# GpSimd issues its 32 row gathers in groups of four, and waits for the fourth's landing before it begins the next group

## The chip, the core and the metric

The kernel runs on one core of a Trainium2 chip. A core has a matrix engine (TensorE, PE in the profile), a vector engine (VectorE, DVE), a scalar engine (ScalarE, ACT), GpSimd (POOL) and SyncE (SP); each has its own instruction stream, and they wait for one another by semaphores. Sixteen DMA engines move data between the core's memory and the chip's main memory. The metric is the device time of one execution in microseconds (us); less is better.

## The reference

The function is one decoder layer on x of 4 x 256 tokens, 256 wide, in float32:

```
x = x + attention(layernorm(x))          # 16 heads of 128, weights = codes * scales
x = x + routed_mlp(layernorm(x), token)  # one of 4 experts, chosen by the token's id
x = x + moe(layernorm(x))                # below

scores  = sigmoid(xs @ router_w.T)
_, idx  = top_k(scores + bias, 4)                 # 4 of 32 experts for each of 1024 tokens
w       = scores[idx] / sum(scores[idx])
out     = sum over experts e of  mlp_e(xs) * w_e  # silu(x@wg) * (x@wu) @ wd, 256 -> 128 -> 256
out     = out + shared_mlp(xs)
```

The change lies in the last part, the mixture of 32 experts. It computes the experts only on the rows that chose them: 1024 tokens x 4 choices = 4096 rows.

## The kernel before, in words

The expert part is sorted by expert. The normalised tokens are stored in main memory as `h_dram`. The table `source` says for each of the 4096 places, in the order of the experts, which token stands there. GpSimd fetches the rows with 32 indirect DMAs (`ROWS = 32`), 128 rows of 256 floats (128 KB) each; I call them row gathers, numbered 0 to 31. Each goes to one of eight slots (`STEPS = 8`) of the tile `xg`, which shares its memory with `x_in`, so the profile calls it `x_in`. Each slot has a semaphore `d_g[n % 8]`, and a landed gather adds 16 to it.

TensorE takes the rows two gathers at a time: `turn_rows(p)` waits until gathers 2p and 2p + 1 have landed, turns them with four transposes (line 1386), and adds 1 to `t_x` after each gather. I call p a pair, 0 to 15. ScalarE copies the turned pair to `xT_all` (`row_copy`, line 1708). Gather n writes over the slot of gather n - 8, so GpSimd waits ahead of gather n for `t_x >= n - 7`.

The experts run as 24 steps b (`NB = 24`), each of 4 x 64 rows. For a step, VectorE copies the rows it needs (`unit_copies`, line 2113) and the weights of the odd experts (`gate_weights`, line 2121). TensorE does the gate and up products (`gate_up_unit`, lines 1399 and 1401, which count up `t_gu`); ScalarE does the silu (line 1652); VectorE multiplies (line 1982); TensorE turns the result (line 1411) and does the down product (lines 1422 and 1425); ScalarE copies it out (line 1662), and SyncE stores it to `y_dram`. Pairs 0 and 1 are turned ahead of the steps, and the table

```
TURN_PAIRS = {0: (2,), 1: (3,), 2: (4,), 3: (5,), 4: (6,), 5: (7, 8), 6: (9,), 7: (10, 11), 8: (12,), 9: (13, 14), 10: (15,)}
```

says behind which step TensorE turns which pairs. TensorE goes through its list in order, so a pair that isn't there holds up the steps behind it.

GpSimd's own list behind the row gathers: eight gathers of `x_all` from `x2_dram` (line 877; the profile calls the source `x_dram`). The first waits for the store that SyncE issues at its step 6, and each for a count of `t_gu`. Then 32 result gathers of `yg` from `y_dram` (line 898), each of which waits for steps to have finished. At the end VectorE and TensorE sum four results per token.

Of the kernel before, what the change touches and what calls it, by code (L numbers as in the profile page):

```python
# [45 lines left out]
HALVES = (T * TOPK + NE * (HS - 1)) // HS + 1  # L46
UNITS, NB = HALVES // 2, HALVES // 4
STEPS = 8
PACK = 4
ROWS = T * TOPK // SLOTS  # L50
PAIRS_OF_ROWS = ROWS // 2
# [2 lines left out]
HOT = NT // 2  # L54
assert NB * PACK == HALVES == 96 and STEPS == 2 * PACK and (2 * NB - 3) % 3 == 0
CH = TOPK * NT
# [6 lines left out]
def wait(eng, sem, value):  # L63

    if isinstance(value, int) and value <= 0:
        return
    eng.wait_ge(sem, value)


def apart(eng):  # L70


    eng.nop(nofuse=True)
# [132 lines left out]
def decoder_layer(nc, a, out):  # L206
    ctx = ExitStack()
    with ctx:
# [3 lines left out]
        def sem(name):  # L212
            return ctx.enter_context(nc.semaphore(name))
# [236 lines left out]
        t_x, v_x = sem("t_x"), sem("v_x")  # L450
        d_g = [sem(f"d_g{u}") for u in range(STEPS)]
        d_y = [sem(f"d_y{u}") for u in range(3)]
# [230 lines left out]
        def _(pool):  # L683
# [183 lines left out]

            for n in range(ROWS):
                wait(pool, t_x, n - STEPS + 1)
                pool.indirect_dma_start(out=xg[:, n % STEPS, :], out_offset=None, in_=h_dram,  # L870
                                        in_offset=bass.IndirectOffsetOnAxis(ap=source[:, n:n + 1], axis=0),
                                        bounds_check=T - 1, oob_is_err=False).then_inc(d_g[n % STEPS], 16)

# [120 lines left out]
        def _(pe):  # L994
# [163 lines left out]

            at = [pe.alloc_register(f"at{i}") for i in range(STEPS)]

            def load_kinds(w):

                apart(pe)
                pe.reg_load(at[w % 2 * PACK:w % 2 * PACK + PACK],
                            seg_expert[0:1, :, :].rearrange("p h i -> p (h i)")[:, w * PACK:(w + 1) * PACK])

# [195 lines left out]
            def load_experts(word):  # L1362

                for i in range(2):
                    into = at[i * PACK:(i + 1) * PACK] if word == 0 else ahead[(2 * word - 2 + i) * PACK:(2 * word - 1 + i) * PACK]
                    apart(pe)
                    start = 2 * i * NB + word * PACK
                    pe.reg_load(into, column_of[0:1, start:start + PACK])

# [922 lines left out]
```

## Time and profile before

| | |
|---|---|
| median of 3 runs | 535.88 us (534.71 to 536.13) |
| the profiled execution, its own time | 529.36 us |
| its span, from first to last instruction | 527.6 us |
| around the span | 1.76 us |
| granted TensorE clock, mean | 0.968 of full speed |
| TensorE busy | 476.5 us, 90% |
| VectorE busy | 386.4 us, 73% |
| ScalarE busy | 290.9 us, 55% |
| GpSimd busy | 203.0 us, 38% |
| the DMA queue of GpSimd's gathers and scatters | 3936 packets, 10.55 MB, 6.8% of 16 engines |

The profiled execution is 6.5 us shorter than the median of the timed runs, so a difference that is worked out from the trace is added to the median, and the trace's own total isn't compared with it. Busy time is not the same as need: each engine works through its list, and what matters is which wait ends last at each place. A time in square brackets in a row is idle time ahead of an instruction, with what ended it; "remote" and "another core or an unknown queue" mean that the profile knows no instruction of this kernel that ended it. The row gathers lie between 380 and 435 us of the span, the `x_all` gathers between 438 and 449, the result gathers between 457 and 512.

### The profile page before, as it was taken

The page shows a single profiled execution, that of the slowest core. Times are in us where ns is not written, and L with a number is a line of the kernel's source. Part 1 is how long each engine was busy: PE and PEld are TensorE (multiplying, and loading weights), DVE is VectorE, ACT ScalarE, POOL GpSimd, SP SyncE. Part 2 cuts the span into 40 slices and gives each one's busy share as a digit, 9 for nine tenths or more (in the row PEclk, how much of TensorE's full clock was granted, in tenths as well). Part 3 has the DMA queues.
Part 4 walks back from the last instruction along what each step waited for, and adds up shares of the span by engine and source line. Part 5 has one row for each costly group of instructions (what it writes and reads, how often), then busy time and mean ns, then how long its engine had stood idle before and what let it go on. Part 6 is the DMA issues. An engine that isn't in the chain of part 4 may idle for free.

```text
span 527.6 us, 11508 instructions
## 1 busy us (share of the span) xinstructions
PE 476.5 (90%) x3407; PEld 403.4 (76%) x3407; DVE 386.4 (73%) x997; ACT 290.9 (55%) x750; POOL 203.0 (38%) x248
## 2 busy tenths in 40 slices
PE   6899999999999999999999999899867988848848
PEld 6688999998998999999999998798734554424425
DVE  5689979879889879789888886887936863525415
ACT  2677667656667656667566655564323544423332
POOL 4418604404305215124122245253174655265250
PEclk9999999999999999999999999999996999987888
DMA  7342211201202203102005912999732455243334
GB/s 195 117 115 60 71 31 33 79 19 53 74 2 61 69 0 84 45 26 74 0 0 180 329 47 85 253 311 295 222 101 70 141 163 179 94 140 111 110 119 141
DMA packets 60662, 56.72 MB, mean 107 GB/s; under 512 B 4896, under 2 KB 57968, under 8 KB 60528
## 3 DMA queue, kind: packets, MB, share of 16 engines
q1 hardware_dynamic: 55984, 45.18, 28.8%
q0 software_dynamic: 3936, 10.55, 6.8%
q10 hardware_dynamic: 704, 0.52, 0.3%
q8 instruction: 18, 0.29, 0.2%
q14 instruction: 20, 0.16, 0.1%
HBM read 45.72 MB, written 16.81 MB: 119 GB/s over the span
## 4 chain that ended last, share of the span: by engine, by line
PE 72%; DVE 8%; another core or an unknown queue 6%; issue 5%; ACT 3%; POOL 3%; DVEq 1%; DMA 1%; ACTq 1%; SPq 0%; POOLq 0%
PE bank L997 18%; PE bank L998 17%; PE bank L999 17%; PE bank L1078 5%; PE bank L1399 4%; PE bank L1422 3%; PE bank L1003 1%; PE bank L1475 1%; POOL h_row L748 1%; DVE gate_of_odd L2121 1%; PE bank L1411 1%; PE bank L1425 1%; PE bank L1386 1%; POOL xs_dram L817 1%
## 5 line engine op out<-in xcount | busy, mean ns | idle before, releaser
L708 POOL TENSOR_TENSOR w_lo<-st_c,w_hi 128x512 fp32r<-128x512 f32 x32 | 41.4, 1293 | 175.1 <-ACT w_hi L1488 175.1
L1525 ACT ACTIVATE prob<-bank,nmax 128x256 f32<-128x256 f32 x128 | 59.6, 471 | 74.2 <-DVE nmax L1810 73.7
L1399 PE MATMUL bank<-moe_w,xT 128*64 x192 | 51.9, 411 | 16.2 <-DVE gate_of_odd L2121 15.1
L1810 DVE TENSOR_REDUCE nmax<-bank 128x2 f32<-128x512 f32 x64 | 44.1, 689 | 23.8 <-PE bank L999 23.8
L1825 DVE TENSOR_SCALAR prob<-prob,rinv 128x256 f32<-128x256 f32 x128 | 57.6, 491 | 2.3
L1802 DVE SCALAR_TENSOR_TENSOR qk_lo<-bank,b_col,qk_hi 128x512 fp32r<-128x512 f32 x64 | 47.7, 745 | 14.5 <-ACT qk_hi L1517 14.5
L1517 ACT ACTIVATE qk_hi<-bank,b_col 128x512 fp32r<-128x512 f32 x64 | 44.0, 688 | 22.1 <-PE bank L999 20.9
L997 PE MATMUL bank<-hT_hi,w_lo 128*128 128x512 f32 x128 | 51.3, 401 | 1.4 <-DVE qk_lo L1802 1.2
L1399 PEld LDWEIGHTS bank<-moe_w,xT 128*64 128x64 f32 x192 | 25.4, 145 | 35.3 <-issue 26.6
L1401 PE MATMUL bank<-gate_of_odd,xT 128*64 128x256 f32 x192 | 51.9, 411 | 0.2 <-issue 0.2
L998 PE MATMUL bank<-hT_lo,w_hi 128*128 128x512 f32 x128 | 50.7, 396 | 0.0
L999 PE MATMUL bank<-hT_hi,w_hi 128*128 128x512 f32 x128 | 50.4, 394 | 0.0
L870 POOL DMA_INDIRECT x_in<-h_dram,source x32 | 33.1, 1034 | 39.1 <-DVE source L2065 18.1
L1982 DVE TENSOR_TENSOR hid<-bank,sg 128x256 f32<-128x256 f32 x24 | 10.1, 421 | 50.2 <-ACT sg L1652 43.1
L1832 DVE TENSOR_TENSOR pT_lo<-bank,pT_hi 128x512 fp32r<-128x512 f32 x64 | 43.5, 680 | 0.6 <-ACT pT_hi L1542 0.6
L898 POOL DMA_INDIRECT yg<-y_dram,y_slot x32 | 30.7, 959 | 31.7 <-issue 20.6
L705 POOL TENSOR_TENSOR st_c<-st_c,st_s 128x512 f32<-128x512 f32 x32 | 41.8, 1305 | 1.3
L997 PE MATMUL bank<-pT_hi,v_lo 128*128 128x256 f32 x128 | 41.1, 321 | 0.5 <-DVE oT_lo L1840 0.5
L1422 PE MATMUL bank<-moe_w,hidT 128*64 x96 | 29.5, 439 | 10.5 <-issue 7.7
L1542 ACT CAST pT_hi<-bank 128x512 fp32r<-128x512 f32 x64 | 38.1, 595 | 0.7 <-PE bank L1078 0.7
L1078 PE MATMUL bank<-ident,prob 128*128 128x128 f32 x256 | 38.4, 272 | 0.0
L997 PE MATMUL bank<-qk_hi,qk_lo 128*128 128x256 f32 x128 | 36.6, 286 | 0.8 <-DVE qk_lo L1802 0.8
(288 smaller groups left out, 1546.1 us busy)
## 6 DMA issues: line engine op xcount, KB each, us to landing
y_dram<-ysb SPq DMA_DIRECT2D x24, 256.0 KB
moe_w<-in_w_gate SPq DMA_DIRECT2D x8, 512.0 KB, 8.3
moe_w<-in_w_up SPq DMA_DIRECT2D x8, 512.0 KB, 7.8
moe_w<-in_w_down SPq DMA_DIRECT2D x4, 1024.0 KB, 8.7
st_c<-in_wq_codes SPq DMA_DIRECT2D x16, 128.0 KB
st_c<-in_wk_codes SPq DMA_DIRECT2D x16, 128.0 KB
st_c<-in_wv_codes SPq DMA_DIRECT2D x8, 256.0 KB
st_c<-in_wo_codes SPq DMA_DIRECT2D x8, 256.0 KB
```

The lines of the kernel that those rows point to most:

```text
L997: pe.matmul(o, l_lo, r_hi, start=start, stop=False, skip_group_check=share)
L998: pe.matmul(o, l_hi, r_lo, start=False, stop=False, skip_group_check=share)
L999: return pe.matmul(o, l_hi, r_hi, start=False, stop=stop, skip_group_check=share)
L1078: mm = pe.transpose(bP[i % 2][:, kt * S + qt * P:kt * S + qt * P + P], prob[:, i % 4, qt, kt * P:kt * P + P], ident[:, :])
L1399: pe.matmul(o[0:HS, :], rows[:, 0:HS], weights_of(even_expert(b, i), kt * 2 * FI, 2 * FI), start=kt == 0, stop=kt == KT - 1, skip_group_ch ...
L1401: mm = pe.matmul(o[HS:SLOTS, :], rows[:, HS:SLOTS], gate_of_odd[:, (2 * b + i) % 3, kt * 2 * FI:(kt + 1) * 2 * FI], start=kt == 0, stop=kt ...
L1422: pe.matmul(o[0:HS, :], columns[:, 0:HS], weights_of(even_expert(b, i), 2 * D, D), start=True, stop=True, skip_group_check=True)
L1517: act.activation(qk_hi[:, hp, m, n * HALF:(n + 1) * HALF], src[:, :], ACT.Identity, bias=b_col[:, bass.ds(g_h + m * H, 1)]).then_inc(a_qk, 1)
L1525: ex = act.activation(prob[:, i % 4, qt, :], bS[i % 2][:, qt * S:(qt + 1) * S], ACT.Exp, bias=nmax[:, i % 2, qt:qt + 1], scale=-1.0, accum ...
L1802: dve.scalar_tensor_tensor(out=qk_lo[:, hp, m, n * HALF:(n + 1) * HALF], in0=src[:, :], scalar=b_col[:, bass.ds(g_h + m * H, 1)], in1=qk_h ...
L1810: dve.tensor_reduce(nmax[:, i % 2, :], bS[i % 2][:, :].rearrange("p (q k) -> p q k", q=2), AX.X, ALU.min).then_inc(v_max, 1)
L1825: sc = dve.tensor_scalar(prob[:, j % 4, qt, :], prob[:, j % 4, qt, :], rinv[:, j % 2, qt:qt + 1], None, ALU.mult)
```

## The change

The gathers are issued in the same order, from the same engine, to the same slots. Before gathers 4, 8, 12, 16, 20, 24 and 28, GpSimd now also waits until the gather right ahead (3, 7, 11, ...) has landed. That makes seven new waits. The `x_all` gathers and the result gathers have no new wait.

```
@@
 STEPS = 8
+BURST = 4
 PACK = 4
@@
             for n in range(ROWS):
                 wait(pool, t_x, n - STEPS + 1)
+                if n and n % BURST == 0:
+                    pool.wait_ge(d_g[(n - 1) % STEPS], 16 * ((n - 1) // STEPS + 1))
                 pool.indirect_dma_start(out=xg[:, n % STEPS, :], out_offset=None, in_=h_dram,
                                         in_offset=bass.IndirectOffsetOnAxis(ap=source[:, n:n + 1], axis=0),
                                         bounds_check=T - 1, oob_is_err=False).then_inc(d_g[n % STEPS], 16)
```

## Rows read from the trace of the kernel before

**Rows 1.** Page, part 4: the chain that ended last, shares of the span.
```profile
PE 72%; DVE 8%; another core or an unknown queue 6%; issue 5%; ACT 3%; POOL 3%; DVEq 1%; DMA 1%; ACTq 1%; SPq 0%; POOLq 0%
```
**Rows 2.** Chain, 388 to 400 us and 425 to 427: start, length, what.
```profile
388.97 9.18 another core or an unknown queue
...
399.54 0.68 PE bank L1399
400.24 0.41 PE bank L1399
...
425.94 0.20 PE bank L1399
```
**Rows 3.** Timeline of GpSimd: start, length, line, operation [idle before].
```profile
380.78 1.20 POOL L870 DMA_INDIRECT x_in<-h_dram,source  x1 [18.09 <-DVE source L2065]
...
384.89 1.00 POOL L870 DMA_INDIRECT x_in<-h_dram,source  x1 [0.30 <-issue]
386.20 1.00 POOL L870 DMA_INDIRECT x_in<-h_dram,source  x1 [0.30 <-issue]
...
395.34 1.00 POOL L870 DMA_INDIRECT x_in<-h_dram,source  x1 [0.30 <-issue]
398.94 1.00 POOL L870 DMA_INDIRECT x_in<-h_dram,source  x1 [2.60 <-remote]
...
429.96 1.00 POOL L870 DMA_INDIRECT x_in<-h_dram,source  x1 [1.51 <-PE bank L1386]
...
433.87 1.00 POOL L870 DMA_INDIRECT x_in<-h_dram,source  x1 [0.30 <-issue]
438.80 0.97 POOL L877 DMA_INDIRECT x_all<-x_dram,dest  x1 [3.93 <-DMA x_dram<-x_all]
...
447.60 0.95 POOL L877 DMA_INDIRECT x_all<-x_dram,dest  x1 [0.30 <-issue]
...
479.58 0.95 POOL L898 DMA_INDIRECT yg<-y_dram,y_slot  x1 [0.30 <-issue]
...
510.71 0.95 POOL L898 DMA_INDIRECT yg<-y_dram,y_slot  x1 [0.30 <-issue]
```
**Rows 4.** Timeline of ScalarE.
```profile
449.56 0.59 ACT L1708 COPY xT_all<-bank 128x512 f32<-128x512 f32 x1 [3.91 <-remote]
...
481.58 0.38 ACT L1652 ACTIVATE sg<-bank 128x256 f32<-128x256 f32 x1 [4.38 <-remote]
...
513.44 0.38 ACT L1652 ACTIVATE sg<-bank 128x256 f32<-128x256 f32 x1 [7.36 <-remote]
```
**Rows 5.** Timeline of TensorE's weight loads (the second half of pair 1).
```profile
387.80 0.20 PEld L1386 LDWEIGHTS bank<-ident,x_in 128*128 128x128 f32 x2 [0.44 <-DMA x_in<-h_dram,source]
```
**Rows 6.** Timeline of TensorE's matmuls: pair 2, pairs 7 and 8, pairs 13 and 14.
```profile
390.81 0.66 PE L1386 MATMUL bank<-ident,x_in 128*128 128x128 f32 x4
...
418.06 1.04 PE L1386 MATMUL bank<-ident,x_in 128*128 128x128 f32 x8
...
437.19 1.04 PE L1386 MATMUL bank<-ident,x_in 128*128 128x128 f32 x8
```
**Rows 7.** Windows: us, PE, PEld, DVE, ACT, POOL busy (x), PEclk, DMA share, GB/s.
```profile
386.00:391.00 5.00, 4.01 (x30) 2.43 (x29) 3.52 (x13) 2.08 (x5) 3.89 (x4) 1.00 0.36 104
...
394.00:395.00 1.00, 0.00 (x0) 0.00 (x0) 0.00 (x0) 0.00 (x0) 0.96 (x1) 1.00 0.41 119
...
404.00:405.00 1.00, 1.00 (x8) 0.62 (x6) 0.96 (x3) 0.00 (x0) 0.69 (x2) 0.50 0.00 0
...
431.00:436.00 5.00, 4.64 (x41) 2.56 (x39) 1.42 (x7) 2.48 (x7) 3.00 (x3) 1.00 0.81 263
```
**Rows 8.** Timeline of SyncE: the store that the `x_all` gathers wait for.
```profile
431.85 0.36 SPq L669 DMA_DIRECT2D x_dram<-x_all  x1
```
**Rows 9.** DMA issues of the page: operation, count, KB each, us to landing.
```profile
x_dram<-x_all SPq DMA_DIRECT2D x1, 1056.0 KB, 6.7
```
**Rows 10.** Timeline of VectorE: the table of the gathers.
```profile
379.67 0.19 DVE L2065 TENSOR_SCALAR source<-bank 128x32 int32<-128x32 f32 x1 [0.19 <-PE bank L1346]
```

More of the change, by code:

```diff
@@ L48 @@
 STEPS = 8
+BURST = 4
 PACK = 4
@@ L869, in _ @@
                 wait(pool, t_x, n - STEPS + 1)
+                if n and n % BURST == 0:
+                    pool.wait_ge(d_g[(n - 1) % STEPS], 16 * ((n - 1) // STEPS + 1))
                 pool.indirect_dma_start(out=xg[:, n % STEPS, :], out_offset=None, in_=h_dram,
```

## The prediction, as put on record before the changed kernel ran

> **What bounds the kernel now.** I read the chain of waits first. TensorE has 72% of it, and 6% is "another core or an unknown queue" [rows 1]. A piece of that kind lies right where the row gathers run: ScalarE does nothing for 9.18 us from 388.97, then does its first silu, VectorE multiplies, and TensorE can go on at 399.54 [rows 2]. No instruction of the kernel ends this stall. So I looked at what ends beside it.
>
> GpSimd's timeline shows twelve row gathers in an unbroken row, from 380.78 until the twelfth, which begins at 395.34 and takes 1.00 us; then it too is idle for 2.60 us until a "remote" event [rows 3]. ScalarE wakes at 388.97 + 9.18 = 398.15, that is 1.8 us after GpSimd stopped. The same shape returns three times. ScalarE begins at 449.56 after 3.91 us of "remote" idleness, and the last `x_all` gather ended at 447.60 + 0.95 = 448.55; it begins at 481.58, a group of result gathers ended at 480.53; it begins at 513.44, the last result gather ended at 511.66 [rows 3, 4]. So ScalarE wakes 1.0, 1.05 and 1.8 us after a run of gathers stops. My reading is that something that ScalarE needs from memory, most likely its next block of instructions, doesn't come while GpSimd issues gathers back to back, and comes in a pause. The rows show the coincidence, not the cause.
>
> **The price of one new wait.** Back to back, gathers begin 1.31 us apart (384.89 to 386.20) [rows 3]. Gather 3 begins at 384.89, and TensorE, which waited for it, begins at 387.80 [rows 3, 5]. So a row gather lands 2.9 us after its start. This was beside 104 GB/s of traffic; later the gathers share the engines with stores, up to 263 GB/s and a DMA share of 0.81 [rows 7], and I take 3.0 on the mean. For the upper end, nothing shows a gather's landing there; I take one us more, 3.9.
>
> From the landing to the next gather's start, two rows bound the price. The store of 1056 KB was issued at 431.85 and took 6.7 us to land, so at 438.55, and GpSimd began at 438.80: 0.25 us [rows 3, 8, 9]. The table `source` was ready at 379.67 + 0.19 = 379.86, and GpSimd began at 380.78: 0.9 us [rows 3, 10]. I take 0.5, since the first of the two is itself a wait on a landing. A group of four then takes 3 x 1.31 + 3.0 + 0.5 = 7.4 us. With both low ends it is 3.9 + 2.9 + 0.25 = 7.1, with both high ends 3.9 + 3.9 + 0.9 = 8.7.
>
> The Trainium skill ("DMA: Bandwidth & Descriptors", Anatomy of one DMA) puts a DMA from GpSimd at about 2.0 us plus bytes over 436 GB/s, which for 128 KB is an estimate of 2.3 us. The row has 2.9 from the start of the issue, and the sum goes by the row. By the page, a group would take 6.7 us and the whole would end near 530.
>
> **The new timetable of the gathers.** Gather 4 begins at 384.89 + 2.9 + 0.5 = 388.3 instead of 386.20 [rows 3]. The further groups begin 7.4 us apart: 395.7 (gather 8), 403.1, 410.5, 417.9, 425.3 and 432.7 (gather 28). Before, gather 28 began at 429.96 and gather 31 at 433.87 [rows 3]; now gather 31 begins at 432.7 + 3.9 = 436.6, which is 2.7 later. The old waits on `t_x` ask for pairs that TensorE turned long ago by then and add nothing.
>
> **What the early part gains.** The pause after gather 7 lasts from 388.3 + 3.9 + 1.0 = 393.2 to 395.7. If ScalarE wakes 1.8 us into a pause, it wakes at 395.0 instead of 398.15: 3.2 us earlier. Pair 2 (gathers 4 and 5) now lands at 388.3 + 1.3 + 2.9 = 392.5 instead of being turned at 390.81 [rows 6], but TensorE then waits for ScalarE in any case, so this is hidden; without that cover it would cost 1.7 us.
>
> The clock adds to it. It was full at 394 to 395 and half (0.50, so 1.2 GHz) at 404 to 405, after TensorE had been idle [rows 7]; the pieces of line 1399 took 0.41 us there and 0.20 at full clock [rows 2]. TensorE does about nine such steps and six transposes between 399.54 and 405. A shorter idle time may spare the fall: 9 x 0.21 + 6 x 0.1 = 2.5 us. So TensorE could be 3.2 to 5.7 us early when it comes to the later pairs.
>
> **Where that gain ends.** Two places hold it back, both by the timetable.
>
> First, TensorE's turns. Pair 8 needs gather 17, which lands at 410.5 + 1.3 + 3.0 = 414.8, and was turned in the second half of the row at 418.06: 3.8 us of slack. Pair 14 needs gather 29, which lands at 432.7 + 1.3 + 3.0 = 437.0. It was turned in the second half of the row at 437.19, so from 437.7 [rows 6]. The slack is 0.7 us. However early TensorE is, it gets past pair 14 only 0.7 us earlier than before.
>
> Second, the `x_all` gathers, which stand behind gather 31 in GpSimd's list. The store that they wait for would come early too, but GpSimd is free at 436.6 + 1.0 + 0.3 = 437.9. They begin 0.9 us earlier than at 438.80 [rows 3] and take as long as before. ScalarE's stall that ended at 449.56 ended 1.0 us behind them [rows 4], so it ends 0.9 earlier. Behind it, each step and the result gathers move as one.
>
> The sum: up to 5.7 us gained at 400, of which 5 are given back by 438, and 0.8 us remain. On the profiled execution's own time that is 529.36 - 0.8 = 528.6 us; the median lies 6.5 us above that execution, and I put the difference on it: 535.88 - 0.8 = 535.1 us. A difference within 0.3% (1.6 us) is no change that a measurement of this kernel can tell, so this forecast is "no change".
>
> **Rival 1, faster: the groups follow one another quickly.** With 7.1 us per group, gather 28 begins at 388.0 + 6 x 7.1 = 430.6. Gather 29 lands at 434.8, so pair 14 comes 2.9 us earlier, and the `x_all` gathers begin at 435.8, 3.0 earlier. Time: 532.9 us. For it: the low ends are both from waits on landings. Against it: the stores. A stronger form is that one of ScalarE's later stalls, such as the 3.91 us [rows 4], also gets shorter because its fetch falls in another pause: up to 530 us.
>
> **Rival 2, slower: the chain of landings gets longer than TensorE's need.** The place is pair 14 and the first `x_all` gather; it decides once a group takes more than about 7.55 us, since then 388.3 + 6 x 7.55 + 5.2 passes 438.8. With a landing of 3.4 and a wake of 0.7 a group takes 8.0 us. Gather 28 begins at 388.5 + 48 = 436.5, gather 29 lands at 441.2 (3.5 us late), and the `x_all` gathers begin at 441.7 (2.9 late). Time: 535.9 + 3.1 = 539.0 us; at 8.7 us per group it would be 543. For it: the DMA share of 0.81 around 433 [rows 7], and nothing else that limits the last groups.
>
> **Rival 3: a pause doesn't end ScalarE's stall.** Then it lasts to 398.15 as before, the groups' waits are covered by the slack of 0.7 us and more, and the time stays at 535.9 us, or some tenths above. For it: GpSimd's own 2.60 us of "remote" idleness [rows 3] could have the same foreign cause as ScalarE's stall, instead of being its end. The Trainium skill ("DMA: Bandwidth & Descriptors", Queues, rings and completion order) speaks for this rival: each DMA engine takes turns between its queues packet by packet, so that a fetch wouldn't have to wait for the gathers to pause. By that page nothing is gained at 389. The four coincidences above speak against it.
>
> **Chances.** The forecast, a gain that the timetable takes back: 0.35, no change. Rival 1: 0.33, faster. Rival 2: 0.22, slower. Rival 3: 0.10, of which I count 0.04 as no change and 0.06 as slower. Together faster 0.33, same 0.39, slower 0.28. The forecast's own range is 534.3 to 537.4. The whole range takes in most of rival 1, down to 530.5, and rival 2 up to a group of 8.2 us, 540.0.
>
> **What would show it.** In the changed kernel, GpSimd's gathers should stand in groups of four, the groups 7.4 us apart, with pauses of 2.5 us. ScalarE's long stall should end at 395, near the end of the second group, instead of at 398.15, and the clock may stay full through it. TensorE should then wait for a row gather at pair 14, near 437. The first `x_all` gather should begin near 438 with GpSimd, not the store, as its last wait. The forecast is wrong if the groups are 7.1 us apart or less and the gain of the early part survives, if they are 8 us apart and TensorE waits for gathers at several pairs, or if the later stalls of ScalarE change their length by themselves.

## The result: slower, and outside the predicted range

The changed kernel takes 540.12 us (median of four runs, 537.47 to 541.99); the runs of the kernel before beside them have a median of 535.3 us (529.9 to 536.13). The comparison's ratio, changed to before, is 1.0148 with a 95% interval of 1.0108 to 1.0187 (the quotient of the two medians is 1.009; slower both ways). The prediction was 535.1 us, "no change", with a range up to 540.0, so the median passed the upper end by 0.12 us.

The profiled execution of the changed kernel took 541.99 us (span 540.3), that of the kernel before 529.36 (span 527.6). These two lie 12.6 us apart, more than the kernels do by the ratio, so a part of their distance is the scatter of runs. Lines after the change stand three further down: L870 is now L873, L877 is L880, L1386 is L1389.

GpSimd's timeline of the changed kernel (start, length, line, operation, idle time before). The first rows are gathers 0 and 3, then the first gather of each further group, with the last of a group where I need it, then the first and last `x_all` gather.
```profile
381.66 1.20 POOL L873 DMA_INDIRECT x_in<-h_dram,source  x1 [19.54 <-DVE column_of L2083]
...
385.78 1.12 POOL L873 DMA_INDIRECT x_in<-h_dram,source  x1 [0.31 <-issue]
389.42 1.00 POOL L873 DMA_INDIRECT x_in<-h_dram,source  x1 [2.51 <-DMA x_in<-h_dram,source]
...
398.70 1.07 POOL L873 DMA_INDIRECT x_in<-h_dram,source  x1 [4.28 <-PE bank L1389]
...
406.49 1.00 POOL L873 DMA_INDIRECT x_in<-h_dram,source  x1 [2.80 <-DMA x_in<-h_dram,source]
...
415.08 1.00 POOL L873 DMA_INDIRECT x_in<-h_dram,source  x1 [3.31 <-DMA x_in<-h_dram,source]
...
422.73 1.00 POOL L873 DMA_INDIRECT x_in<-h_dram,source  x1 [2.66 <-DMA x_in<-h_dram,source]
...
430.87 1.00 POOL L873 DMA_INDIRECT x_in<-h_dram,source  x1 [2.60 <-PE bank L1389]
...
434.79 1.00 POOL L873 DMA_INDIRECT x_in<-h_dram,source  x1 [0.30 <-issue]
441.36 1.00 POOL L873 DMA_INDIRECT x_in<-h_dram,source  x1 [5.58 <-PE bank L1389]
...
446.58 0.96 POOL L880 DMA_INDIRECT x_all<-x_dram,dest  x1 [0.30 <-issue]
...
455.66 0.95 POOL L880 DMA_INDIRECT x_all<-x_dram,dest  x1 [0.30 <-issue]
```
The groups begin 7.76, 9.28, 7.79, 8.59, 7.65, 8.14 and 10.49 us apart; from gather 4 to gather 28 that is (441.36 - 389.42) / 6 = 8.66 us a group, where the prediction had 7.4. Gather 28 begins at 441.36 instead of 429.96, and the `x_all` gathers at 446.58 instead of 438.80 [rows 3]. The last wait of a group is put down to "PE bank L1389" in three rows. TensorE had been done with those buffers; the landing is what was late, as the chain shows.

The chain of waits of the changed kernel (start, length, what): landings on the path to the end.
```profile
385.78 2.88 DMA x_in<-h_dram,source
...
393.43 4.46 DMA x_in<-h_dram,source
...
416.38 3.09 DMA x_in<-h_dram,source
...
434.79 5.76 DMA x_in<-h_dram,source
...
446.20 5.76 another core or an unknown queue
...
452.01 6.44 another core or an unknown queue
```
The longest interval can be read in full: gathers 24 to 27 are issued in 434.79 - 430.87 = 3.92 us, the last lands 5.76 us after its start, at 440.55, and gather 28 begins 0.81 us behind that: 10.49 us. After gather 3 the same reads 385.78 + 2.88 = 388.66, and 0.76 us to 389.42. The page of the profile has DMA at 5% of the chain, where it was 1% [rows 1].

TensorE's turns in the changed kernel (pair 2, second half of pair 3, first half of pair 8, first half of pair 14):
```profile
393.21 0.84 PE L1389 MATMUL bank<-ident,x_in 128*128 128x128 f32 x4 [1.47 <-DMA x_in<-h_dram,source]
...
397.93 0.44 PE L1389 MATMUL bank<-ident,x_in 128*128 128x128 f32 x2 [1.42 <-DMA x_in<-h_dram,source]
...
418.33 0.41 PE L1389 MATMUL bank<-ident,x_in 128*128 128x128 f32 x2 [2.44 <-DMA x_in<-h_dram,source]
...
444.41 0.66 PE L1389 MATMUL bank<-ident,x_in 128*128 128x128 f32 x2 [3.39 <-DMA x_in<-h_dram,source]
```
Before, pairs 7 and 8 were one row of eight turns without a wait, and so were pairs 13 and 14 [rows 6]. Both rows are torn apart now. The view of waits of the changed kernel, from 375 us to 540, says how much in all (us, times, longest):
```profile
PE bank L1389 <- DMA x_in<-h_dram,source: 14.4, 13, 3.4
```
Before, TensorE's matmuls had no such wait, and its weight loads one of 0.44 us [rows 5].

ScalarE in the changed kernel:
```profile
391.83 0.38 ACT L1655 ACTIVATE sg<-bank 128x256 f32<-128x256 f32 x1 [2.07 <-PE bank L1404]
...
451.99 0.38 ACT L1655 ACTIVATE sg<-bank 128x256 f32<-128x256 f32 x1 [5.22 <-remote]
...
493.05 0.39 ACT L1655 ACTIVATE sg<-bank 128x256 f32<-128x256 f32 x1 [12.79 <-remote]
```
The 9.18 us stall [rows 2] is gone altogether, others came: "remote" idleness of ScalarE sums to 39.8 us after 375 us, 42.3 before. The windows of the changed kernel (columns as in [rows 7]) show that the clock no longer falls there, that it falls later, and how busy the DMA engines are when gather 27 lands:
```profile
395.00:400.00 5.00, 3.04 (x26) 1.74 (x24) 4.31 (x16) 1.84 (x5) 1.07 (x1) 1.00 0.11 30
...
420.00:425.00 5.00, 4.70 (x22) 2.56 (x23) 1.09 (x6) 0.97 (x2) 2.04 (x3) 0.50 0.19 52
...
435.00:440.00 5.00, 4.01 (x30) 2.16 (x30) 2.65 (x13) 3.54 (x10) 0.78 (x1) 1.00 0.89 295
```
At 420 to 425 us TensorE runs at half clock (0.50, so 1.2 GHz). The clock fell at 419.0, between its two waits for pair 8 (2.44 us ahead of 418.33, 1.04 us ahead of 419.78), and was full again at 426. The twelve products of one expert step (lines 1402 and 1425 in the chain) begin over 4.74 us (420.77 to 425.51); the same twelve at full clock take 2.53 us (403.32 to 405.85). The kernel before had the full clock in this stretch. So the fall that the prediction hoped to spare came later in the kernel, at a price of 2.2 us.

To place gain and loss I compared when VectorE begins the product of each expert step (L1982, now L1985) in the two traces. The changed kernel is 6.4 us early at step 0, 3.6 to 3.9 early at steps 3 to 5, level at step 6 (behind pair 8), 1.8 late at step 9, and 11.8 late at step 10 (behind pair 14). It ends 12 late. So there was an early gain, gone behind pair 8, and a loss behind pair 14. This pair of traces can't price pair 14: the product of step 10 follows the silu at 451.99, so the 5.22 us stall ahead of it is in the ten us, and it is none of the waits' doing that I can show. Traces without such stalls have to say it.

### The profile page after: what moved, and what is told of

It is laid out like the page before. It is cut to its first block, busy times and chain, and to the rows that moved or that the text cites. A ratio compares the mean times of both kernels' runs of the same rounds, so it can differ in the third digit from the quotient of the medians.

```text
span 540.3 us, 11514 instructions
## 1 busy us (share of the span) xinstructions
PE 480.0 (89%) x3407; PEld 403.8 (75%) x3407; DVE 386.2 (71%) x997; ACT 290.3 (54%) x750; POOL 203.9 (38%) x248
## 4 chain that ended last, share of the span: by engine, by line
PE 70%; another core or an unknown queue 7%; DVE 6%; DMA 5%; issue 4%; POOL 4%; ACT 2%; ACTq 0%; DVEq 0%; SPq 0%; POOLq 0%
PE bank L1000 17%; PE bank L1001 17%; PE bank L1002 16%; PE bank L1081 5%; PE bank L1402 4%; DMA x_in<-h_dram,source 4%; PE bank L1425 3%; POOL x_in L873 1%; PE bank L1006 1%; PE bank L1478 1%; POOL h_row L749 1%; PE bank L1414 1%; PE bank L1404 1%; PE bank L1389 1%
## 5 line engine op out<-in xcount | busy, mean ns | idle before, releaser
L1402 PE MATMUL bank<-moe_w,xT 128*64 x192 | 52.7, 419 | 12.9 <-DVE gate_of_odd L2124 10.5
L1520 ACT ACTIVATE qk_hi<-bank,b_col 128x512 fp32r<-128x512 f32 x64 | 44.0, 688 | 22.1 <-PE bank L1002 20.9
L1985 DVE TENSOR_TENSOR hid<-bank,sg 128x256 f32<-128x256 f32 x24 | 10.1, 423 | 60.1 <-ACT sg L1655 57.2
L873 POOL DMA_INDIRECT x_in<-h_dram,source x32 | 33.6, 1049 | 50.6 <-DVE column_of L2083 19.5
```

The source lines that it names most:

```text
L1402: pe.matmul(o[0:HS, :], rows[:, 0:HS], weights_of(even_expert(b, i), kt * 2 * FI, 2 * FI), start=kt == 0, stop=kt == KT - 1, skip_group_ch ...
L1520: act.activation(qk_hi[:, hp, m, n * HALF:(n + 1) * HALF], src[:, :], ACT.Identity, bias=b_col[:, bass.ds(g_h + m * H, 1)]).then_inc(a_qk, 1)
```

## The experiments

Ratios are time over that of the kernel before on the same chip, with 95% intervals. The chips differ. On the first, the kernel before has a median of 531.87 us, with stalls of ScalarE that no instruction of the kernel ends, as in the traces above. On the chips of the other runs it takes 495.7 to 496.1 us, and its trace has no such stall at all. Each edit is shown against the kernel before, unless said otherwise.

**Which waits cost, on the chip with the stalls.** Three kernels have a part of the waits, or a pause without a wait for a landing; the fourth waits for a landing that is nearly always past.
```
e1   if n in (4, 8): pool.wait_ge(d_g[(n - 1) % STEPS], ...)
e2   if n in (12, 16, 20, 24, 28): the same
e3   if n in (4, 8): two pool.tensor_tensor(nt1, var, minus_half, ALU.pow)
e4   if n >= 4: pool.wait_ge(d_g[(n - 4) % STEPS], ...)
```


> Only the waits before gathers 4 and 8 stand; the five later ones are gone. Theory A (a pause of GpSimd ends ScalarE's stall early; the five later waits are what costs): ScalarE's 9.2 us stall near 389 is gone as in the changed kernel, the later gathers are issued on time, and the kernel takes no longer than before, 532 to 536 us. Theory B (any wait on a landing costs about its own length at the end, wherever it stands): two sevenths of the loss, about 537 us. Theory C (ScalarE's stall falls where it likes, pauses don't matter): the stall is still there in this run, 535 to 536 us.

> Only the waits before gathers 12, 16, 20, 24 and 28 stand. Theory A: the 9.2 us stall of ScalarE near 389 is back, the groups from gather 12 on are 8 to 9 us apart, and the first x_all gather begins 6 to 8 us later than before; 539 to 543 us, as slow as the changed kernel or slower, since the early gain is missing. Theory B: five sevenths of the loss, about 539 us. Theory C: as slow as the changed kernel, with or without the stall.

> No wait on a landing. Ahead of gathers 4 and 8, GpSimd does two small power operations of about 1 us each (on spare data), so that it pauses in issuing for some 2.5 us. Theory A (the pause matters, not the landing): ScalarE's stall near 389 is gone or ends by 396, and the time is that of the kernel with the two waits, within 1.5 us. Rival (it is the empty queue that matters, so that a landing must have been seen): the gathers ahead have landed 2.9 us after their start, about when the pause ends, so the stall is shortened only in part. Theory C: no effect on the stall.

> Before each gather n from 4 on, GpSimd waits for the landing of gather n - 4: at most four are in flight, but there is no pause, since a gather lands 3 to 4 us after its start and four are issued in 5.2 us. Theory A (pause): the stall of ScalarE near 389 stays at about 9 us, the gathers come at 1.3 us as before, and the time is that of before, 534 to 537 us. Rival (the number in flight is what holds the fetch up): the stall gets shorter than 5 us, with the gathers still 1.3 us apart.

Measured: e1 533.01 us, 1.0027 [0.9989, 1.0065]; e2 533.91, 1.0014 [0.9975, 1.0054]; e3 536.77, 1.0086 [1.0039, 1.0133]; e4 531.95, 0.9982 [0.9952, 1.0012]. Two and five waits each cost 0.3% or less here, with intervals that reach 0.7%, so neither part alone makes the loss on this chip. Two expectations failed: e2 was to take 539 to 543 us, and e3 was to take as long as e1 within 1.5 us, while it took 3.8 us more.

On the stall, ScalarE's timeline in e1:
```profile
391.27 0.38 ACT L1654 ACTIVATE sg<-bank 128x256 f32<-128x256 f32 x1 [2.10 <-PE bank L1403]
...
411.63 0.38 ACT L1654 ACTIVATE sg<-bank 128x256 f32<-128x256 f32 x1 [6.59 <-remote]
```
Two pauses, and the early stall is gone; another comes at 411.63. The same engine in e4:
```profile
398.79 0.38 ACT L1654 ACTIVATE sg<-bank 128x256 f32<-128x256 f32 x1 [9.24 <-remote]
```
The stall of 6.59 us in e1 began within a row of ten gathers and ended 1.3 us behind it. In e4, whose gathers stay 1.3 us apart, the stall is as it was. e3 has the pauses (3.43 us of pow work) without a wait for a landing, and its early stall is gone as well. These three agree that a pause, whatever makes it, removes the stall. But e2 has a counterexample; its ScalarE:
```profile
396.26 0.38 ACT L1654 ACTIVATE sg<-bank 128x256 f32<-128x256 f32 x1 [6.14 <-remote]
```
and its GpSimd at that time:
```profile
395.42 1.00 POOL L872 DMA_INDIRECT x_in<-h_dram,source  x1 [0.30 <-issue]
396.73 1.00 POOL L872 DMA_INDIRECT x_in<-h_dram,source  x1 [0.30 <-issue]
```
The stall ended in the middle of an unbroken row of gathers. The changed kernel's 5.22 us stall did so too, at 451.99, while `x_all` gathers were being issued. The trace of the kernel before has such a case as well, which the prediction's four coincidences leave out: a stall of ScalarE of 6.92 us, the third longest after 380 us, that ended between two result gathers 1.25 us apart:
```profile
472.10 0.59 ACT L1662 COPY ysb<-bank 128x512 f32<-128x512 f32 x1 [6.92 <-remote]
...
472.25 0.95 POOL L898 DMA_INDIRECT yg<-y_dram,y_slot  x1 [0.30 <-issue]
```
Moving a stall away is supported by the runs; that the pause ends it is not settled.

**The price by itself, on chips without the stalls.**
```
e5    the changed kernel
e6    if n and n % BURST == 0 and n != 28
e7    if n and n % BURST == 0: wait for the landing of gather n - 2, not n - 1
e8    kernel before, and ahead of the x_all gathers five pow operations on GpSimd
```


> The changed kernel once more, as the measure for the others on this chip. Every theory: 1.0 to 1.9% slower than before. In its profile the groups again begin 7.7 to 10.5 us apart, ScalarE's stall near 389 is gone, and the first x_all gather begins 6 to 8 us later than in the kernel before.

> The changed kernel without its last wait (before gather 28). Theory D (the series of landings outlasts the slack only at its end, where gather 27 lands beside the 1 MB store of x_dram in 5.8 us): gather 28 is issued 1.3 us behind gather 27, TensorE's wait for pair 14 shrinks from 3.4 us to under 1, the first x_all gather begins 4 to 6 us earlier than in the changed kernel, and at least half of the loss is gone: 0 to 0.8% over before. Rival E (the loss comes from the series as a whole, every wait its share): 6/7 of the loss stay, 1.0 to 1.4% over before.

> As changed, but at the seven places the wait is for the landing of the third gather of the group instead of the fourth. A group then takes 3.9 us of issue plus 2.4 us instead of 3.7 us of pause, so 7.1 to 7.4 us. Theory D and the threshold of 7.55 us per group of the prediction: the loss shrinks to 0 to 0.5%, while ScalarE's stall near 389 stays gone, since the pauses are still over 2 us. Rival E: five sevenths of the loss, about 1.0%. Rival F (a pause ends the stall only if the queue has run empty): the stall is back and over 5 us long.

> The kernel before, with about 8 us of small power operations on GpSimd between the last row gather and the first x_all gather, so that TensorE gets its pairs on time but the x_all gathers are late. The first x_all gather begins 3 to 6 us later than before (it waited 3.9 us there for a store). Theory G (the lateness of the x_all gathers is what the end pays): 3 to 6 us slower, 0.6 to 1.1%. Rival H (the pairs' lateness is what the end pays, and the x_all and result gathers have slack behind them): within 0.4% of before.

Measured: e5 509.46 us, 1.0257 [1.0227, 1.0286]; e6 507.67, 1.0234 [1.0199, 1.0269]; e7 503.24, 1.0151 [1.0116, 1.0187]; e8 499.58, 1.0074 [1.0049, 1.0098]. Without a stall to remove, the waits cost more than on the first chip: 2.6% instead of 1.5%. Without the last wait, the longest of the seven, the loss is 0.2 points smaller, which lies within the two intervals; the expectation that at least half would go failed. Waiting for the third's landing shortens a group to 7.3 us and takes off 1.1 points, so shorter groups cost less. But e7's expectation failed too: below the 7.55 us of the prediction the loss was to be 0 to 0.5%. That threshold belongs to the chip with the stalls. On these chips TensorE turned pair 14 at about 428.3 in the kernel before (e10, below). With gather 4 at 388.8 as in e5, and 1.3 + 3.0 us from gather 28 to the landing of gather 29, a group may take (428.3 - 4.3 - 388.8) / 6 = 5.9 us, an estimate, and 7.3 us is above that. In e8 only the `x_all` gathers are late, by 8.35 us (436.62) against the trace of the kernel before on such a chip, and the time rises by 3.5 us. So that lateness is not hidden, but less than half of it comes through. VectorE in e8 shows where:
```profile
448.23 0.32 DVE L2202 TENSOR_SCALAR y_kt<-x_all 128x32 f32<-128x32 f32 x1 [5.33 <-DMA x_all<-x_dram,dest]
```

**Where on the path, in traces of the same kind of chip.** The kernel before and the changed kernel were run again for their traces, with e7 once more, and the same rule on the other gathers.
```
e10   the kernel before
e11   the changed kernel
e12   as e7
e13   kernel before; x_all gathers in two fours, result gathers in fours,
      each four behind the landing of the one before
```


> The kernel before, unchanged, for a trace from the same chip as the others of this group. Two levels of time have been seen for it, 532 and 496 us, on different chips. Every theory: 1.00 times before. If the chip is one of the first kind, ScalarE's stalls of 3 to 13 us with no releaser in the kernel are there; if of the second, there are none over 2 us.

> The changed kernel. Theory J (the series of groups costs about 13 us wherever it runs, and on a chip of the first kind some 5 to 6 us of it are earned back, because the pauses shorten ScalarE's stall near 389): 1.4 to 1.9% slower on a chip of the first kind, 2.3 to 2.9% on one of the second. Rival K (the loss is the same on both): 2.0% in either case.

> As changed, but with the waits on the landing of the third gather of each group. Theory J: on a chip of the first kind the smaller loss (7 us instead of 13 on the other chip) is just about earned back by the stall: 0.995 to 1.005 of before. On the second kind 1.015 as measured. Rival K: 1.015 on both.

> The row gathers as before; instead the x_all gathers are issued in two groups of four and the result gathers in groups of four, each group behind the landing of the one before. Theory L (on a chip of the first kind ScalarE's stall ends 1 to 2 us into any pause of GpSimd): its stalls behind 440 us, up to 7.4 us in the kernel before, are all under 5 us, each ending inside a pause; the time is 0.97 to 1.00 of before. On a chip of the second kind there is nothing to shorten, and the waits cost 0 to 1.5%. Rival M (the pauses don't matter): the stalls keep their lengths, 1.00 to 1.02.

Measured: e10 495.66 us, 1.0004 [0.998, 1.0028]; e11 509.87, 1.0298 [1.0259, 1.0338]; e12 503.6, 1.0152 [1.0114, 1.0189]; e13 515.57, 1.039 [1.0349, 1.043]. GpSimd in e10 (gather 28, the last row gather, the first of `x_all`):
```profile
421.11 1.00 POOL L870 DMA_INDIRECT x_in<-h_dram,source  x1 [3.17 <-PE bank L1386]
...
425.02 1.00 POOL L870 DMA_INDIRECT x_in<-h_dram,source  x1 [0.30 <-issue]
428.27 0.96 POOL L877 DMA_INDIRECT x_all<-x_dram,dest  x1 [2.25 <-DMA x_dram<-x_all]
```
GpSimd is ahead of its readers, and the `x_all` gathers wait for the store. TensorE's turns of pairs 13 and 14 in e10, with no wait for a gather:
```profile
427.75 1.04 PE L1386 MATMUL bank<-ident,x_in 128*128 128x128 f32 x8
```
GpSimd in e11 (gather 27, gather 28, the first of `x_all`):
```profile
433.66 1.00 POOL L873 DMA_INDIRECT x_in<-h_dram,source  x1 [0.30 <-issue]
439.35 0.99 POOL L873 DMA_INDIRECT x_in<-h_dram,source  x1 [4.70 <-DMA x_in<-h_dram,source]
...
444.69 0.97 POOL L880 DMA_INDIRECT x_all<-x_dram,dest  x1 [0.30 <-issue]
```
Gather 28 begins 18.2 us later than in e10. TensorE's turns in e11, of pairs 8, 13 and 14:
```profile
417.17 0.50 PE L1389 MATMUL bank<-ident,x_in 128*128 128x128 f32 x2 [3.26 <-DMA x_in<-h_dram,source]
...
436.64 0.44 PE L1389 MATMUL bank<-ident,x_in 128*128 128x128 f32 x2 [2.50 <-DMA x_in<-h_dram,source]
...
443.49 0.44 PE L1389 MATMUL bank<-ident,x_in 128*128 128x128 f32 x2 [0.82 <-DMA x_in<-h_dram,source]
```
Now the row gathers are the late ones, TensorE waits for them at each of these pairs, and the `x_all` gathers wait for GpSimd alone. Step by step against e10, e11 is 1.9 to 2.5 us late up to step 5 (1.6 of it was there before the first gather, at which the two kernels do the same), 7.5 at step 6, 9.0 at step 8, 12.3 at step 9, 15.1 at step 10 and 15.1 at the end. The loss enters at pair 8 and at pairs 13 and 14, and nothing is added behind the `x_all` gathers. In the windows of 432 to 437 us TensorE was busy 5.00 of 5 us in e10 and 2.18 in e11.

The loss has a second part, the clock. Windows of e10 and e11, in this order:
```profile
436.00:441.00 5.00, 5.00 (x48) 2.99 (x42) 2.33 (x10) 2.83 (x9) 2.32 (x3) 1.00 0.64 189
...
436.00:441.00 5.00, 4.36 (x26) 2.55 (x26) 1.58 (x7) 0.97 (x2) 1.34 (x2) 0.68 0.32 106
```
TensorE in e10 has the full clock from 380 us to the last step. In e11 it is at half clock behind its waits for pair 8 (from 417.4 to 424.2) and behind those for pair 13 (from 437.7 to 441.3). The twelve products of a step, which begin over 2.42 us in e10, take 4.75 us in the first stretch and 3.98 in the second: 3.9 us more. TensorE's waits for gathers at pairs 8, 13 and 14 sum to 7.6 us. Together that is 11.5 of the 12.6 us by which e11 falls back between steps 5 and 10. No run holds the clock still, so this split is read from the traces and not tested.

e13 shows that the rule costs more still on gathers whose reader stands right behind: VectorE waits 22.1 us for result gathers there, in six waits, against 5.3 us in three in e10.

**Do the waits add up, and what lengthens a landing?** By then it was open whether each wait has a price of its own, and why one landing took 5 us.
```
e14   as e1            e15   as e2
e16   changed kernel, SyncE's store x_dram<-x_all at n == 8 instead of n == 6
e17   changed kernel, BURST = 8
```


> Only the waits before gathers 4 and 8 (as e1). If this chip shows no foreign stalls of ScalarE (before at 496 us), the timetable from the changed kernel's rows has gather 8 about 5 us late and the rest 1.3 us apart until the slots hold them, so gather 17 lands at about the time at which TensorE asks for it: 0 to 0.5% slower. If every wait cost its share: 0.8%. On a chip of the first kind (before at 532): 0.997 to 1.007 as measured there.

> Only the waits before gathers 12 to 28 (as e2). Without foreign stalls, the groups begin near 400, 408, 416, 424 and 432; gather 29 lands near 437 where TensorE asks for it near 430: 1.2 to 1.8% slower, so two thirds of the loss or less, and more than e14's by far. If every wait cost its share: 2.1%. On a chip of the first kind: 0.997 to 1.006 as measured there.

> The changed kernel with SyncE's 1 MB store to x_dram issued at its step 8 instead of 6. If the long landing of gather 27 (5 to 6 us) comes from this store beside it, the last group begins some 7.8 us behind the one before instead of 9.6 to 10.9, and the loss shrinks by 0.2 to 0.4 points; if not, it stays at 2.6 to 3.0% without foreign stalls.

> As changed, but in groups of eight, with waits before gathers 8, 16 and 24. A group of eight takes 9.1 us of issue and 3.7 us of pause, 1.6 us per gather against 2.1 in fours and 1.3 before. Without foreign stalls gather 29 is issued near 426 to 428, late by less than 2: 0.2 to 0.9% slower. If the number of waits decided: 3/7 of the loss, 1.2%.

Measured: e14 498.47 us, 1.0047 [1.0013, 1.0081]; e15 505.15, 1.0169 [1.0104, 1.0234]; e16 510.47, 1.0268 [1.0214, 1.0322]; e17 499.71, 1.0068 [1.0033, 1.0102]. Two waits and five waits make 0.47 + 1.69 = 2.2% apart and 2.6 or 3.0% together. The intervals of the two sum to some 0.7 points either way, so on these chips it isn't shown that the parts fall short of the whole. On the chip with the stalls they do: 0.27 + 0.14 = 0.4% apart against 1.5% together, if the chips of the two measurements are alike. My reading is that a part of the first two waits is covered by the slack ahead of pairs 8 and 14, and that this slack is then missing for the five behind them; no run tests that by itself. Groups of eight, with three waits, cost 0.7%.

In e16 the 1056 KB store is out of the way of the last landing. GpSimd in e16:
```profile
434.07 1.00 POOL L873 DMA_INDIRECT x_in<-h_dram,source  x1 [0.31 <-issue]
438.02 1.03 POOL L873 DMA_INDIRECT x_in<-h_dram,source  x1 [2.94 <-DMA x_in<-h_dram,source]
```
and SyncE's store there:
```profile
440.49 0.36 SPq L670 DMA_DIRECT2D x_dram<-x_all  x1
```
Gather 27 lands 3.13 us after its start, where it took 5.76 in the changed kernel's first trace (store issued at 432.90), 4.88 in e11 (store at 431.41) and 6.18 in e5 (store at 433.15). The store is the one thing that e16 moved, so I take it for the cause of that long landing. It gained no time that can be measured: the `x_all` gathers wait for the later store instead and begin at 445.71. Long landings come without this store too: 4.46 us for gather 7 in the changed kernel, and 5.28 us for gather 15 (408.83) in e16. What lengthened those is open.

No variant was faster than the kernel before; e4 is equal to it within its interval.

## Why the prediction was wrong

**The step that failed: the price of one new wait, 7.4 us a group.** Of its three terms two were too small, the landing above all. The issues took 3.9 to 4.1 us, about as predicted. The landing was put at 3.0 on the mean, from one row beside 104 GB/s of traffic [rows 5, 7]. In quiet stretches it was 2.7 to 3.1, but 4.46 after gather 7 and 5.76 beside the store. Over the six groups it was 3.9 us on the mean (8.66 less 4.0 of issue and 0.8 of wake), the prediction's upper bound. From landing to next issue 0.76 and 0.81 us were measured, where I took 0.5 between 0.25 and 0.9. The low end, 0.25 us [rows 3, 8, 9], was a difference against a landing time that the page of the profile rounds to a tenth, and no later row shows a wake that short. With 3.93 + 3.0 + 0.8 = 7.73 even a quiet group passes the 7.55 us at which the prediction's own timetable tips over. The mean was 8.66, at the high bound of 8.7. Two numbers pointed to the upper half: the DMA share of 0.81 around 433 [rows 7], and the 0.9 us behind the table [rows 10]. I chose low in both.

The Trainium skill ("DMA: Bandwidth & Descriptors", Anatomy of one DMA) led to an estimate of 2.3 us for such a transfer. The shortest landing piece in a chain was 2.52 us, the usual one 2.7 to 3.1, and beside the store it was 5.76, two and a half times the estimate. The Trainium skill ("DMA: Bandwidth & Descriptors", Queues, rings and completion order) has a DMA engine take turns between its queues packet by packet. e16 agrees with that as far as it goes, since the landing took 3.13 us instead of 4.88 to 6.18 once the store's packets were elsewhere.

**The timetable.** Gather 4 was put at 388.3 and came at 389.42; gather 28 at 432.7 and came at 441.36; the `x_all` gathers at 437.9 and came at 446.58. Six groups at 1.26 us too little are 7.6 of the 8.7 us, and 0.9 us were there at the first gather (381.66 after 380.78).

**The early gain.** Right in direction, and too small at first: 3.2 to 5.7 us were predicted, 6.4 measured at step 0 and 3.6 to 3.9 three steps on. The stall did not end at 395 but did not happen, and the clock stayed full until pair 8. That a new wait of TensorE brings a fall of the clock of its own, 2.2 us behind pair 8, has no term in the prediction. That TensorE's wait for pair 2 is hidden by ScalarE's stall was wrong for that reason: with the cover gone TensorE waited 1.47 us at 393.21.

**Where the gain ends.** The two places were right as places where the series is late: pair 14, and the `x_all` gathers. On the chips without stalls nothing was added at the second. A third was passed over: pair 8 had 3.8 us of slack in the timetable, and longer groups with an early TensorE used it up (2.44 us of waiting at 418.33). The `x_all` gathers had GpSimd, not the store, as their last wait, as predicted.

**Rival 2 is what happened**, with its mechanism and with its place as one of two, pair 8 being the other. Its threshold was not tested on the chip that it was worked out for. For 8.7 us a group it said 543 us, 7.1 more than before; with 8.66 the ratio makes it 0.0148 x 535.9 = 7.9 more. I gave it 0.22 and sized it at 8.0 us a group. **Rival 1** is out, since the shortest interval in the changed kernel's three traces was 7.55 us (414.25 to 421.80 in e11). **Rival 3** is out for the stall at 389, which went away here, in e1 and in e3. Its doubt was fair all the same: e2's stall ended without a pause. What these stalls are stays open. Gathers back to back do not suffice, since the chips of e10 have the same gathers and no stall.

**What the ratio of the two kinds of chip says.** Where there is no stall to remove, the waits cost 2.6 to 3.0%; with the stalls 1.5% (0.9% by the medians). By the ratios that is 12.8 and 14.8 us against 7.9, so 5 to 7 us apart, about the size of the early gain (6.4 us at step 0, 3.6 to 3.9 at steps 3 to 5). That is a comparison across chips, and supports the account rather than proves it.

## What to carry to other kernels

Before a producer is made to wait for landings, work out its rate with the wait in it (issues, a landing beside the heaviest traffic of that stretch, and the wake) and hold it against the rate of the reader: here the reader left some 7.55 us a group on one chip and some 5.9 on others, and the intervals were 7.6 to 10.5. A slack is spent once, by all waits together, so the price of several waits need not be the sum of the prices of each. Count the clock in as well: a wait that stops TensorE for 3 to 4 us cost another 1.6 to 2.3 us at half clock behind it here. And before a stall is bought off, see whether it is there on another chip: this one was worth some 5 to 7 us on one and was not there on the next.

## What the runs showed of the hardware

- The same kernel takes 532 to 536 us on some chips and 496 on others. On the slow kind, ScalarE has stalls of up to 12.79 us that no instruction of the kernel ends. On the fast kind there is none. Some of these stalls end while GpSimd issues gathers 1.3 us apart (6.92 us in the kernel before, 5.22 in the changed kernel, 6.14 in e2), so a pause of GpSimd isn't needed for their end.
- A gather of 128 rows (128 KB) lands 2.7 to 3.1 us after its start in quiet stretches, and 4.88 to 6.18 us after it beside a store of 1056 KB (295 GB/s in that window, with 5.76 us).
- GpSimd began 0.76 to 0.81 us after the landing that it waited for.
- The granted clock of TensorE fell to half (0.50) at 419.0 in the changed kernel, and at 417.4 and 437.7 in e11, each time at waits that stopped TensorE for 2.8 to 4.0 us in all. It stayed there for 3.6 to 6.8 us. Twelve products began over 4.74 us instead of 2.53.
